# First attention by heads of 64: unmerged weights, scores on row halves, attention on column halves

## What is computed

```python
x = x + tanh(g_xattn[0]) * L0_xattn(ctx, _layernorm(x), mask, ...)   # 16 heads of 64
x = x + tanh(g_ffn[0]) * L0_ffn(_layernorm(x), ...)                  # butterfly weights, 512 wide
x = x + tanh(g_xattn[1]) * L1_xattn(_layernorm(x), ctx, ...)         # 16 heads of 8, top 32 of 77
x = x + tanh(g_ffn[1]) * L1_ffn(_layernorm(x), ...)                  # one of 8 experts per token
```

```python
xn = layer_norm(x, g1, b1);  ln_lat = layer_norm(latents, g2, b2)    # x: the context, latents: the tokens
q = ln_lat @ Wq                                                      # 128 -> 16 heads x 64
k, v = split(concatenate([xn, ln_lat], axis=1) @ Wkv)                # 77 + 128 = 205 rows
weight = softmax(where(mask, (q * scale) @ (k * scale).T, -max))
out = (weight @ v).reshape(b, l, 1024) @ Wout
```

## Time and profile before

| | us |
|---|---|
| median of 3 runs | 796.79 |
| lowest, highest | 795.46, 798.51 |
| the profiled execution | 796.77 |
| its span | 795.0 |
| TensorE busy in it | 717.2 (90%) |
| VectorE busy | 574.9 (72%) |
| ScalarE busy | 463.9 (58%) |
| GpSimd busy | 452.4 (57%) |

### The profile page before, as it was taken

The page is one execution under the profiler, slowest core; times in us unless marked ns, Lnnn a source line. Parts: engine busy times, 40 slices in busy tenths (PEclk is TensorE's granted clock), DMA queues, the critical chain, the costliest instruction groups (busy, mean ns, idle before and its releaser), DMA issues.

```text
span 795.0 us, 17992 instructions
## 1 busy us (share of the span) xinstructions
PE 717.2 (90%) x4442; PEld 575.6 (72%) x4442; DVE 574.9 (72%) x3758; ACT 463.9 (58%) x1226; POOL 452.4 (57%) x705
## 2 busy tenths in 40 slices
PE   5899989999999999999999999999999965752896
PEld 5766677778787877777787787777877854541886
DVE  2755525788887979797888887879788899964222
ACT  2265567686767676767677676768576734220221
POOL 6275747665665747474847565656566445642243
PEclk9689999999999999999999999999999985555799
DMA  6200099930000000000000000000000000101772
GB/s 196 63 1 1 1 292 304 298 113 1 2 2 0 0 0 0 0 0 0 0 0 0 0 0 0 0 0 0 0 1 2 2 0 15 47 15 53 209 219 67
DMA packets 38531, 37.85 MB, mean 48 GB/s; under 512 B 3632, under 2 KB 34247, under 8 KB 38482
## 3 DMA queue, kind: packets, MB, share of 16 engines
q1 hardware_dynamic: 32984, 27.76, 12.7%
q10 hardware_dynamic: 3994, 6.36, 2.8%
q0 software_dynamic: 1504, 3.17, 1.1%
HBM read 16.28 MB, written 21.45 MB: 47 GB/s over the span
## 4 chain that ended last, share of the span: by engine, by line
PE 44%; DVE 30%; ACT 11%; issue 7%; SPq 3%; POOL 2%; DMA 2%; another core or an unknown queue 1%; DVEq 1%; ACTq 0%; POOLq 0%
DVE raw L1537 12%; DVE m L1531 9%; PE bank L854 8%; PE bank L726 6%; PE bank L881 4%; PE bank L842 4%; ACT prob L1188 4%; DVE negmax L1479 3%; PE bank L1160 3%; PE bank L871 3%; PE bank L1170 3%; PE bank L872 2%; ACT raw L1188 2%; PE bank L903 2%; PE bank L940 2%
## 5 line engine op out<-in xcount | busy, mean ns | idle before, releaser
L1537 DVE MATCH_REPLACE8 raw<-m,raw 128x77 f32<-128x77 f32 x1024 | 220.1, 222 | 0.0
L1531 DVE MAX8 m<-raw 128x8 f32<-128x77 f32 x1024 | 189.3, 226 | 1.1 <-DVE raw L1537 0.6
L1188 ACT ACTIVATE prob<-bank,negmax 128x205 f32<-128x205 f32 x256 | 108.3, 428 | 99.0 <-DVE negmax L1479 98.7
L498 POOL TENSOR_TENSOR prob<-prob,inv 128x820 f32<-128x820 f32 x64 | 99.4, 1553 | 64.4 <-DVE inv L1484 64.4
L1479 DVE TENSOR_REDUCE negmax<-bank 128x2 f32<-128x410 f32 x128 | 74.2, 580 | 80.9 <-PE bank L854 79.0
L517 POOL TENSOR_TENSOR raw<-raw,m 128x616 f32<-128x616 f32 x64 | 77.8, 1216 | 93.3 <-DVEq L1513 93.3
L854 PE MATMUL bank<-kvT,g_sb 128*128 128x205 f32 x512 | 123.8, 365 | 0.0
L854 PEld LDWEIGHTS bank<-kvT,g_sb 128*128 128x128 f32 x512 | 83.0, 190 | 10.2
L940 PEld LDWEIGHTS bank<-v,p1T 77*128 77x128 f32 x512 | 73.4, 213 | 14.7 <-issue 4.5
L1537 DVE MATCH_VALUE_LOAD raw<-m,raw 128x8 f32 x1024 | 78.0, 76 | 0.0
L940 PE MATMUL bank<-v,p1T 77*128 (+1 forms) x512 | 70.6, 265 | 8.2 <-ACT p1T L1188 3.9
(11 more groups left out here) (232 smaller groups left out, 1337.7 us busy)
## 6 DMA issues: line engine op xcount, KB each, us to landing
z_sorted<-no_row SPq DMA_DIRECT2D x1, 17415.0 KB, 64.8
b_w<-in_L_ffn_W ACTq DMA_DIRECT2D x23, 256.0 KB
z_tile<-z_sorted SPq DMA_DIRECT2D x23, 129.0 KB, 2.6
w<-in_L_ffn_W SPq DMA_DIRECT2D x8, 256.0 KB, 4.6
raw<-in_L_xattn_Wkv SPq DMA_DIRECT2D x2, 512.0 KB, 5.7
xs<-in_x SPq DMA_DIRECT2D x1, 960.0 KB, 6.9
cx<-in_ctx SPq DMA_DIRECT2D x1, 577.5 KB
raw<-in_L_xattn_Wq SPq DMA_DIRECT2D x1, 512.0 KB, 3.7
```

What stands on the lines that cost most here:

```text
L498: g.tensor_tensor(p, p, inv[:, 4 * q:4 * q + 4].unsqueeze(2).to_broadcast([128, 4, KV]), ALU.mult).then_inc(s["p_norm"], 1)
L1188: return nc.scalar.activation(dst, src, f, **kw)
L1531: v.max(m8[:, h, r, :], sw[:, h, src, :]).then_inc(s[name], 1)
L1537: v.match_replace(sw[:, h, 1, :], m8[:, h, r, :], sw[:, h, src, :], TAKEN)\
```

## The change

- The merged weights a_w and b_w and fourteen setup jobs go. In every step `queries_in` forms q of eight heads (four products of 128 columns on raw Wq, twice a step), `keys_in` k of four heads (two products of 205 columns, four times), `values_in` v of eight heads for the context or for the tokens (one product of 512 columns, four times). They use the banks GZ and OA in turn, and ScalarE copies each out (q_sb, k_sb, v_ctx, v_lat).
- A chunk of 128 partitions holds two heads of 64. `scores` is for a quad of heads: the mask by two products on 64 rows each, and four products of 205 columns on the row halves in turn, the even head of a chunk in bank S0 and the odd one in S1. VectorE takes both maxima of a quad in the even slots, from both banks. The exponentials stay one pair to a slot.
- `attend` writes the two heads of a chunk to the column halves of a bank: eight products of 128 columns for a quad, with 64 columns of weights. ScalarE copies 256 columns instead of 512 (att_T), and `project_out` is eight products at one go.
- copy_keys goes. stage_mask(P) comes, a copy of 128 x 77 in slot 7 on GpSimd.
- Residual and statistics of E (L1491 on rows_out) stand in slot 4 instead of 3, E's r_z inside the top 32 of slot 4, E's reciprocal root in slot 4 on GpSimd. `close_top` stands in slots 1, 3 and 7 behind the residuals and maxima. 12 batches' input statistics move from the setup to step 1, and GpSimd's first roots wait for three batches instead of for all.
- The loads are reordered: the first attention's four weights come after ctx and the second attention's weights.
- The second attention's scores sw and p1 have tiles of their own, as raw has to stay.

The core of the diff:

```diff
-            def project(b, q):
-
-                free("GZ")
+            def queries_in(b, name, j, n):
+
+                dst = (GZ, OA)[name == "OA"]
+                free(name)
                 reach(pe, "kvt_ready", b, 1)
-                for n in range(4):
-                    last = mm(GZ[:, 128 * n:128 * n + 128], a_w[:, 4 * q + n, :], kvT[:, NK:KV], start=True, stop=True)
-                last.then_inc(s["g_psum"], 1)
-                read_next("GZ", "g_ready", 1, q + 1)
+                for c in range(4):
+                    last = mm(dst[:, 128 * c:128 * c + 128], wq_in[:, 512 * j + 128 * c:512 * j + 128 * c + 128],
+                              kvT[:, NK:KV], start=True, stop=True)
...
+            def keys_in(b, name, j, n):
...
+                for c in range(2):
+                    at = 256 * j + 128 * c
+                    last = mm(dst[:, KV * c:KV * c + KV], wkv_in[:, at:at + 128], kvT[:, :], start=True, stop=True)
...
+            def values_in(b, name, rows, j, n):
...
+                mm(dst[0:nr, :], kvT[:, r0:r0 + nr], wkv_in[:, INNER + 512 * j:INNER + 512 * j + 512], start=True, stop=True)\
...
+            def scores(b, q, n):
+
+                reach(pe, "exp_done", b, 2 * q)
+                reach(pe, "w_ready", b, n)
...
+                rows = [slice(0, 64), slice(64, 128)]
+                for u in range(2):
+                    dst = SC[:, u, 0:2 * KV].rearrange("p (h n) -> p h n", h=2)
+                    mm(dst[:, :, 0:NK], ones_rows[rows[u], :],
+                       mask_now[rows[u], :].unsqueeze(1).to_broadcast([64, 2, NK]), start=True, stop=False,
+                       skip_group_check=True)
+                for r in range(2):
+                    for u in range(2):
+                        last = mm(SC[:, u, KV * r:KV * r + KV], q_sb[rows[u], q // 2, 2 * (q % 2) + r, :],
+                                  k_sb[rows[u], q % 2, r, :], start=False, stop=(r == 1), skip_group_check=True)
...
+                for c in range(2):
+                    for v, p, last_part in ((v_ctx, ptc, False), (v_lat, ptl, True)):
+                        for u in range(2):
+                            h = 4 * q + 2 * c + u
+                            last = mm(dst[64 * u:64 * u + 64, 128 * c:128 * c + 128], v[:, DH * h:DH * h + DH],
+                                      p[:, 2 * c + u, :], start=not last_part, stop=last_part, skip_group_check=True)
...
-                    if A is not None:
+                    if A is not None and slot % 2 == 0:
                         maxima(A, slot)
-                    if slot in (1, 5):
-                        close_top()
+                        maxima(A, slot + 1)
...
-                    if slot == 3 and E is not None:
+                    if slot == 4 and E is not None:
                         reach(dve, "o1_psum", E, 1)
                         reach(dve, "xo_added", E, 1)
                         residual(E, last_x(E), M[:, 0:D], 1, "x3_ready")
                         statistics(E, last_x(E), c_st, c_mv, "x3_ready", "c_stats")
...
+                    if slot in (1, 3, 7):
+                        close_top()
```

More of the change, by code:

```diff
@@ L282, in flamingo_kernel, with move_jobs @@
         PLACE_AT[20, 6] = tuple(range(*ROUTES[1]))
-        def job_heads(q):
-            return [8 * (q // 2) + q % 2 + 2 * n for n in range(4)]
-        def job_part(w, q):
-            h0 = job_heads(q)[0]
-            return w[:, h0:h0 + 7:2, :]
         def wait_job(eng, k):
             eng.wait_ge(s["set_act" if k % 2 == 0 else "set_dve"], k // 2 + 1)
-        def move_jobs(eng, jobs, copy, scaled, biased, added=None):
+        def move_jobs(eng, jobs, copy, biased, added=None):
             done = s["set_dve" if jobs[0] % 2 else "set_act"]
@@ L676, in step @@
                     if slot == 4:
+                        if E is not None:
+                            rsqrt(E, c_mv, c_rs, "c_stats", "c_eps", "crs_ready")
                         if A2 is not None:
@@ L767, in _ @@
             last.then_inc(s["set_psum"], 1)
-            pe.wait_ge(s["ld_wout"], 16)
-            wait_job(pe, 4)
-            wait_job(pe, 5)
-            for q in range(QUADS):
-                dst = open_job(J_B + q)
-                for n, h in enumerate(job_heads(q)):
-                    r, c = DH * (h % 2), 128 * (h // 2)
-                    last = mm(dst[:, 128 * n:128 * n + 128], head_rows(2, h), wout_in[r:r + DH, c:c + 128],
-                              start=True, stop=True)
-                last.then_inc(s["set_psum"], 1)
             pe.wait_ge(s["c_perm"], 3 * PST)
@@ L846, in scores @@
-            def scores(b, p):
-                dst = s_bank[p % 2][:, 0:2 * KV].rearrange("p (h n) -> p h n", h=2)
-                reach(pe, "exp_done", b, p - 1)
-                reach(pe, "g_ready", b, p // 2 + 1)
-                apart(pe)
-                mm(dst[:, :, 0:NK], ones_row[:, :], mask_row[:, bass.ds(b, 1), :].to_broadcast([1, 2, NK]),
-                   start=True, stop=False, skip_group_check=True)
-                for n in range(2):
-                    last = mm(dst[:, n, :], g_sb[:, (p // 2) % 2, 2 * (p % 2) + n, :], kvT[:, :],
-                              start=False, stop=(n == 1), skip_group_check=True)
-                last.then_inc(s["s_psum"], 1)
+                for c in range(4):
+                    last = mm(dst[:, 128 * c:128 * c + 128], wq_in[:, 512 * j + 128 * c:512 * j + 128 * c + 128],
+                              kvT[:, NK:KV], start=True, stop=True)
@@ L1127, in step @@
                             probs_T(A, 2)
-                        if A is not None:
-                            scores(A, 7)
+                            values_in(A, "OA", "lat", 1, 9)
                         if B is not None:
@@ L1614, in step @@
                 for slot in range(SLOTS):
-                    if slot in (3, 7) or (slot in (1, 5) and A is None):
-                        close_top()
                     before = slot_before(i, slot) if i is not None else None
@@ L1653, in step @@
                         statistics(E, last_x(E), c_st, c_mv, "x3_ready", "c_stats")
-                    if slot == 4 and E is not None:
-                        reach(dve, "rz_kept", E, 0)
-                        normal(E, last_x(E), r_z, c_mv, c_rs, "crs_ready", "rz_ready")
-                    if slot == 3 and A is not None:
-                        inverses(A, 1)
+                    if slot in (1, 3, 7):
+                        close_top()
                     def between():
@@ L1662, in between @@
                             normal(B, batch(xs, B), b_z, b_mv, b_rs, "brs_ready", "bz_ready")
+                        if slot == 4 and E is not None:
+                            reach(dve, "rz_kept", E, 0)
+                            normal(E, last_x(E), r_z, c_mv, c_rs, "crs_ready", "rz_ready")
                         if slot == 3 and A2 is not None:
                             normal(A2, batch(xs, A2), f_z, f_mv, f_rs, "frs_ready", "fz_ready")
-                        if slot in (1, 5, 7) and A is not None:
+                        if slot % 2 and A is not None:
                             inverses(A, slot // 2)
```

315 lines of the change are left out of this document (164 added, 151 removed).

## The result

| | before | after |
|---|---|---|
| median | 796.66 us | 816.56 us |
| lowest, highest (4 runs each) | 795.46, 798.51 | 815.37, 819.72 |
| span of the profiled execution | 795.0 | 814.5 |
| TensorE busy | 717.2 | 671.9 |
| VectorE, ScalarE, GpSimd busy | 574.9, 463.9, 452.4 | 563.6, 484.5, 448.6 |

The ratio is 1.0254, with an interval of 1.0219 to 1.0289: slower by 20 us. The forecast of 801.3 had the sign, but the time lies outside its range of 781 to 811. TensorE is 45 us lighter, and the kernel is longer all the same.

A forecast was written before the change was run, and what follows sets the result against it. TensorE was taken to bound the kernel before at 37.87 us a step, the ring after at 38.7. 796.8 + 10 (twelve steady steps) - 1 (early steps) - 4.5 (setup) gave 801.3 us, range 781 to 811.

The forecast's parts named there:

- The ring: Steady-step loop from kvT through TensorE, VectorE, GpSimd and ScalarE back to kvT: 38.7 us a step, chance 0.50.
- the GpSimd link: Part of the ring on GpSimd: root of c_mv from 22.9, then staging and below_max, ending at 29.3 us.
- rival 1: Steady step: ring mis-sized by 0.9 us or more, ScalarE behind TensorE binds at 37.0; 781 us, chance 0.20.
- Each link is a dependency or a queue's order, so extra waits add only: Claim on the ring's steady step: the summed 38.7 us can only grow through further waits.
- Setup: Kernel start: fewer setup jobs, roots 3.1 us earlier, twelve batches' statistics moved to step 1; -4.5 us, between 0 and -8.
- Early steps: Four early steps, without c_mv's root ahead of the staging, paced by TensorE and ScalarE; -1 us, between -4 and +2.
- The tail: Kernel end, from 631 us on: keeps its work, 0 +- 1 us.
- TensorE's share: TensorE's own work in a steady step: 34.8 us after the change, or 38.4 with serial columns.
- TensorE sets the pace: Steady step before the change: TensorE bounds the 37.87 us, idling about 0.6 us a step.
- Rival 3: Scores on TensorE: the two row halves don't pair, 39.4 us a step; 809 us, chance 0.12.
- Rival 4: Score banks: exponentials two slots on block a quad's scores, up to 0.5 us a step; 804 to 807, chance 0.15.
- Rival 2: Steady step: TensorE's saving is all kept, 34.8 us a step; 743 us, chance 0.03.

The follow-up runs named there:

- stage_split: Changed kernel with the first four of eight stage_inputs operations put ahead of batch E's reciprocal root on GpSimd; 809.2 us, 1.0134 to before.
- e_slot3: Changed kernel with batch E's residual, statistics and reciprocal root back in slot 3; 798.7 us, 1.0014 to before.
- fill: Changed kernel with 16 idle products of 100 columns added to each step on TensorE where it waits; 804.6 us, 1.0085 to before.
- mask_early: Changed kernel with coefficients and batch 0's mask copy in slot 4 of step 0, roots of batches 1 to 3 in step 1; 808.3 us, 1.0152 to before.
- before_light: Kernel before with eight of sixteen output products of the first attention left out in each step; 787.8 us, 0.9864 to before.

## Why the prediction went wrong

**The ring: right in size, not in what it is made of.** 38.7 forecast, 38.72 measured at full clock, and the links lie within 0.3 us of their forecast places. But stage_split shows that the GpSimd link which the forecast followed was last by 0.3 us only. Close behind it stood another path, by e_slot3 most likely the one through TensorE and ScalarE, priced at 37.0 as rival 1. e_slot3 has it, or what else binds there, at 37.87: third-quad scores at 19.5 and transposes at 24.3 after `down(B)` were right (19.4 and 24.35 there), and from there to kvT e_slot3 has 13.1 us instead of 12.3. The longer step is worth +9.1 over eleven steps, against +10 for twelve in the forecast.

**The step that failed most: the clock.** "Each link is a dependency or a queue's order, so extra waits add only" took TensorE's rates from the earlier trace rows, at a granted clock of 1.00, into a kernel in which TensorE waits. The forecast even says that TensorE will idle 3 to 4 us a step. It idles 4.5 in a step of full clock, and in two steps of three the clock falls to 0.50 on the stretch of TensorE's work with which the ring begins, where that work then takes 5.33 us instead of 3.69. This term is missing from the sum; it is 6 x 1.63 = 9.8 us by the trace of after, and fill, which covers the waits, is 9.6 us shorter in the same steps and 12.0 in the median.

**Setup: -4.5 forecast, 0.0 measured.** The roots did start 4.1 us earlier (28.97 for 33.09), and the first kvT came 9.0 earlier, more than the 3 to 5 forecast, so the loads did not stand in the way. The step that failed is the one not taken: stage_mask stands in the list of the change as a copy in slot 7 and has no term in the sum. What stands ahead of it on GpSimd in step 0 holds the first scores until 39.35; TensorE waits 8.4 us for it. mask_early, with the copy early, has the second kvT 9.9 us sooner.

**Early steps: -1 forecast, +2.4 measured,** between -4 and +2 as bounds. One fall of the clock, at 106.7, lies among them. The rest I did not take apart.

**The tail:** 0 +- 1 forecast, -1.8 measured, not studied. The seventh fall lies in it. By terms the miss is 4.5 (setup) + 3.4 (early) + 8.9 (steady: 9.8 of clock, less 0.9 for the twelfth step, which lies behind the last kvT) - 1.8 = 15.0 us of span. So the clock is the largest term, and setup and early steps together are nearly as large; the 38.7 us of the ring hold.

**TensorE's share.** Forecast 34.8 us of work a step; e_slot3's 136.84 busy of 152.00 us are 34.1. Scores at 1.1 and attention at 1.3 us a quad were near: 0.91 with the masks and 1.02 measured. "TensorE sets the pace" was right by 0.5 us only, by before_light. The idle times of the other engines, 5.6 us on VectorE, did not tell how far the next path was.

**The rivals.** Rival 3 (row halves don't pair) is out by the records. Rival 4 (exponentials block the banks) exists as a wait: TensorE stands 1.18 to 1.22 us before the third quad's scores for ScalarE's exponentials in after as in e_slot3; what it costs alone was not tried. Rival 2 was far out. Two slips in the prediction's own figures change nothing here: its three chances, 0.26, 0.44 and 0.32, add up to 1.02, and the range's upper end of 811 is said to be rival 3's, for which its sum gives 809.

**What stays open:** what decides which step has a fall of the clock, and why e_slot3 loses most of them; why before's second path lies at 37.4 and that of e_slot3 at 37.87. ScalarE's added copy of 0.5 us in slot 7 would fit; no run takes it away.

## What to carry to other kernels

When an engine that was busy 98% of the time is made lighter, ask first how far the next path is (take a piece of its work out and look at the period), and second what its clock does once it waits: price its stretch of the path at the lower clock, too. A new wait costs by where it lies: a copy of 77 columns at the end of a full queue used up all of the 9.0 us that the lighter setup had won. Idle products held the clock here, but they belong only where the wait is longer than they are, and have to be looked at again after every other edit. And a kernel with idle products tells little about who waits for whom: they fill the room that another path would have shown.

## What the runs showed of the hardware

- TensorE's granted clock falls to 0.50 for 3.41 us in a kernel in which TensorE is busy 88% of the time and never waits longer than 1.22 us in a steady step, and a fall costs 1.63 us where it meets the path. Steps with the same waits have it or don't have it. Sixteen idle products a step keep it at 1.00 from 44 us to the tail; five of them in one place don't.
- Products of float32 on the two row halves (64 x 205) run side by side whether the program has them in turn or two by two: their records start 0.004 us apart in the one, up to 0.066 in the other, and a quad takes 0.84 and 0.90 us. On column halves they pair fully in turn (1.02), and half of them with four products of one half in a row (1.52).
